# Attention contexts normalized between two 32x32 block turns on VectorE instead of between TensorE turns

## The reference

```python
def _mha(q, k, v, wq, wk, wv, wo):
    B, S, d = q.shape
    dh = d // H
    qh = (q @ wq).reshape(B, S, H, dh)
    kh = (k @ wk).reshape(B, S, H, dh)
    vh = (v @ wv).reshape(B, S, H, dh)
    scores = jnp.einsum('bqhd,bkhd->bhqk', qh, kh) / jnp.sqrt(jnp.asarray(dh, q.dtype))
    attn = jax.nn.softmax(scores, axis=-1)
    ctx = jnp.einsum('bhqk,bkhd->bqhd', attn, vh).reshape(B, S, d)
    return ctx @ wo
...
for c in range(NUM_NOD):
    ...
    o = _mha(q, k, v, Wq[c], Wk[c], Wv[c], Wo[c])
    nodes[c] = act_w[c] * o + q
...
return _layernorm(out, ln_g, ln_b)
```

## Time and profile before

| | us |
|---|---|
| runs | 2162.97, 2163.7, 2166.92; median 2163.7 |
| the profiled execution, first to last instruction | 2167.6 |
| TensorE busy, matmuls | 2020.1 (93%), 14620 instructions |
| VectorE busy | 1686.2 (78%), 2918 instructions |
| ScalarE busy | 1374.7 (63%), 2687 instructions |
| GpSimd busy | 1112.7 (51%), 1509 instructions |

### The profile page before, as it was taken

How to read it: one execution, slowest core, us unless ns; L and a number is a source line. 1 busy time by engine, 2 the same in 40 slices (tenths; PEclk the granted TensorE clock), 3 DMA queues, 4 the chain that set the end, 5 groups by cost and what they waited for, 6 DMA issues and landing times. The chain is left out here.

```text
span 2167.6 us, 40610 instructions
## 1 busy us (share of the span) xinstructions
PE 2020.1 (93%) x14620; PEld 1506.8 (70%) x14620; DVE 1686.2 (78%) x2918; ACT 1374.7 (63%) x2687; POOL 1112.7 (51%) x1509
## 2 busy tenths in 40 slices
PE   6999999986999995999999988699999999999878
PEld 4677777754887773677777755577877877877745
DVE  5777777765888875777777765499999999999974
ACT  1677777763777773677777653467586685685633
POOL 3555555623767764555555512345736647556423
PEclk8899999997999997999999997899999999999989
DMA  4655566530000003555555515000000000000000
GB/s 133 148 149 147 146 148 149 145 106 1 2 2 2 2 2 78 151 149 146 149 145 150 150 31 200 1 1 1 1 1 1 1 1 0 1 0 1 1 15 20
DMA packets 147750, 144.94 MB, mean 67 GB/s; under 512 B 14048, under 2 KB 106976, under 8 KB 146912
## 3 DMA queue, kind: packets, MB, share of 16 engines
q1 hardware_dynamic: 127968, 132.91, 22.4%
q10 hardware_dynamic: 19584, 9.44, 2.4%
HBM read 94.07 MB, written 38.80 MB: 61 GB/s over the span
## 5 line engine op out<-in xcount | busy, mean ns | idle before, releaser
L606 DVE TENSOR_REDUCE sb_f_mx<-ps_f_s 128x2 f32<-128x512 f32 x768 | 506.4, 686 | 216.5 <-PE ps_f_s L354 215.6
L530 ACT ACTIVATE sb_f_pt<-ps_f_t 128x1024 f32<-128x1024 f32 x384 | 382.1, 1023 | 114.9 <-issue 56.2
L1954 POOL TENSOR_TENSOR sb_mb_h<-sb_mb_h 128x512 f32<-128x512 f32 x128 | 165.0, 1310 | 303.4 <-DVE sb_mb_h L1837 302.3
L354 PE MATMUL ps_f_s<-sb_f_stack 96*128 96x256 bf16 x1536 | 286.5, 279 | 22.1 <-DMA sb_f_stack<-f_scr 14.1
L1832 DVE TENSOR_TENSOR_SCAN sb_mb_h<-sb_mb_da,sb_mb_h 128x1024 f32<-128x1024 f32 x128 | 304.4, 2418 | 2.7 <-ACT sb_mb_da L1692 2.7
L1503 PE MATMUL ps_mb_f<-sb_mb_fc,sb_mb_cw 128*128 128x256 f32 x1280 | 286.8, 381 | 6.7 <-ACT sb_mb_fc L1705 6.6
L1503 PEld LDWEIGHTS ps_mb_f<-sb_mb_fc,sb_mb_cw 128*128 128x128 f32 x1280 | 239.7, 190 | 41.4 <-ACT sb_mb_fc L1705 8.9
L371 PE MATMUL ps_f_t<-sb_f_stack 128*128 128x256 bf16 x1536 | 232.9, 274 | 6.3 <-ACT sb_f_pt L530 3.3
L1692 ACT ACTIVATE sb_mb_da<-sb_mb_dl,sb_mb_an 128x255 f32<-128x255 f32 x512 | 211.0, 496 | 31.3 <-DVE sb_mb_h L1832 30.7
L354 PEld LDWEIGHTS ps_f_s<-sb_f_stack 96*128 96x128 bf16 x1536 | 140.7, 99 | 109.7 <-issue 41.3
L427 PE MATMUL ps_f_a<-sb_f_pt,sb_f_v 128*32 128x256 f32 x3072 | 188.8, 387 | 1.6 <-ACT sb_f_v L579 1.6
(11 more groups left out here) (252 smaller groups left out, 4132.7 us busy)
## 6 DMA issues: line engine op xcount, KB each, us to landing
f_scr<-sb_f_parts SPq DMA_DIRECT2D x96, 384.0 KB, 2.7
sb_f_stack<-f_scr SPq DMA_DIRECT2D x192, 192.0 KB, 3.0
sb_f_stack<-f_scr SPq DMA_DIRECT2D x192, 128.0 KB, 3.1
sb_f_stack<-f_scr SPq DMA_DIRECT2D x192, 64.0 KB, 3.3
sb_f_stack<-sb_f_mrow ACTq DMA_DIRECT2D x96, 96.0 KB
sb_mb_cw<-in_cw SPq DMA_DIRECT2D x1, 5120.0 KB, 19.4
sb_prep_wn<-in_wn SPq DMA_DIRECT2D x6, 512.0 KB, 7.7
sb_m_w<-in_w SPq DMA_DIRECT2D x6, 256.0 KB, 3.1
```

Source lines behind the costliest of these rows:

```text
L354: last = nc.tensor.matmul(s_bank[j % 2][:, h, :], stack[0:ROWS, a.n % STACKS, 0, g * GROUP + pair * 2 + h, half * P:(half + 1) * P], stack ...
L530: nc.scalar.activation(pt[:, e.two, g, half, :, :], t_bank[i % 2][:, :, :], ACT.Exp).then_inc(s["pt_sb"], 1)
L606: nc.vector.tensor_reduce(mx[:, a.two, half, head:head + 2], s_bank[j % 2][:, :, :], AX.X, ALU.max)\
L1954: nc.gpsimd.tensor_tensor(hb[:, c, 0:2, :], hb[:, c, 0:2, :], hb[:, c, 2:4, :], ALU.add).then_inc(s["half_sb"], 1)
```

## The change

The contexts are not turned on TensorE any more. `by_token(u)` on VectorE reads the context bank with one block turn (each 32x32 block by itself) into `ct`, so that the partitions are 32 tokens of each of four heads, and takes the reciprocal of the 16 sums per partition. GpSimd multiplies (`normalize(u)`) into `cn`, and `by_dim(o)` on VectorE turns the blocks back into `cf`. ScalarE's copies `cs` and `cf` and TensorE's `context_tok` and `context_back` are gone. Heads are dealt to slots in another order, so the columns of Wv and the rows of Wo are permuted on the host. The turn of the maxima becomes a plain product with the identity into an fp32 bank. Waits follow the new buffers. A step's item u, not item o of the next step, is now read from the bank.

```diff
-        cs = k.sb(f"{tag}_cs", [P, NG, N], ctx)
-        rsum = k.sb(f"{tag}_rsum", [P, NG, 2, GROUP], ctx)
-        cn = k.sb(f"{tag}_cn", [P, 2, NG, GROUP, DH], ctx)
+        ct = k.sb(f"{tag}_ct", [P, NG, N // SLOT, SLOT], ctx)
+        rsum = k.sb(f"{tag}_rsum", [P, NG, N // SLOT], ctx)
+        cn = k.sb(f"{tag}_cn", [P, N // SLOT, NG, DH], ctx)
...
-        mrow_ps = act_bank[0:MAXROWS, N:N + N // 2].bitcast(BF16)
+        mrow_ps = act_bank[0:MAXROWS, N:2 * N]
...
-                if f.n > OUT_LAG - 1:
-                    pe.wait_ge(s["cn_sb"], f.n - OUT_LAG + 1)
+                if f.n > OUT_LAG:
+                    pe.wait_ge(s["node_sb"], f.n - OUT_LAG)
...
             def values(m, e, o):
 
                 if o:
-                    pe.wait_ge(s["cf_sb"], o.n + 1)
+                    pe.wait_ge(s["ct_sb"], o.n + 1)
                 elif e:
                     pe.wait_ge(s["v_sb"], e.n)
                     if m:
@@ -400,8 +400,9 @@
                 if m:
                     pe.wait_ge(s["mp_sb"], m.n + 1)
                     for half in range(2):
-                        last = nc.tensor.transpose(mrow_ps[:, half * P:(half + 1) * P],
-                                                   mp[:, half, :, :].rearrange("p t h -> p (t h)"), w.identb[:, :])
+                        last = nc.tensor.matmul(mrow_ps[:, half * P:(half + 1) * P],
+                                                mp[:, half, :, :].rearrange("p t h -> p (t h)"), w.identb[:, :],
+                                                start=True, stop=True)
...
-                    pe.wait_ge(s["cf_sb"], u.n)
+                    pe.wait_ge(s["ct_sb"], u.n)
...
-                                                    v[:, u.two, half, g * GROUP + h, :],
+                                                    v[:, u.two, half, h * NG + g, :],
...
-            def context_tok(o):
-
-                pe.wait_ge(s["cs_sb"], o.n + 1)
-                if o.n:
-                    pe.wait_ge(s["node_sb"], o.n)
-                else:
-                    pe.wait_ge(s["qf_sb"], OUT_LAG)
-                for g in range(NG):
-                    for half in range(2):
-                        last = nc.tensor.transpose(mix_bank[:, (2 * g + half) * P:(2 * g + half + 1) * P],
-                                                   cs[:, g, half * P:(half + 1) * P], k.ident[:, :])
-                last.then_inc(s["ct_ps"], 1)
-
-            def context_back(o):
-
-                pe.wait_ge(s["cn_sb"], o.n + 1)
-                for half in range(2):
-                    last = nc.tensor.transpose(act_bank[:, half * P:(half + 1) * P],
-                                               cn[:, half, :, :, :].rearrange("p g h e -> p (g h e)"), k.ident[:, :])
-                last.then_inc(s["cb_ps"], 1)
...
                 if u:
                     scores_t(u, 3)
-                if o:
-                    context_tok(o)
                 if a:
                     scores(a, 0)
...
                     scores_t(e, 1)
-                if o:
-                    context_back(o)
                 if f and step >= EXP_LAG:
                     queries(f)
...
-                if o:
-                    act.wait_ge(s["ctx_ps"], o.n + 1)
-                    if o.n:
-                        act.wait_ge(s["ct_ps"], o.n)
-                    nc.scalar.activation(cs[:, :, :].rearrange("p g n -> p (g n)"), act_bank[:, :], ACT.Copy)\
-                        .then_inc(s["cs_sb"], 1)
+                u = ffn_item(step, SUM_LAG)
                 if u:
                     exponent(u, 3)
...
-                if o:
-                    act.wait_ge(s["cb_ps"], o.n + 1)
-                    if o.n:
-                        act.wait_ge(s["out_ps"], o.n)
-                    nc.scalar.activation(cf[:, :], act_bank[:, 0:N], ACT.Copy).then_inc(s["cf_sb"], 1)
...
-            def normalize(o):
-
-                dve.wait_ge(s["ct_ps"], o.n + 1)
-                ct = mix_bank[:, :].rearrange("p (g a h e) -> p g a h e", g=NG, a=2, h=GROUP)
-                nc.vector.reciprocal(rsum[:, :, :, :], ct[:, :, :, :, SUMROW]).then_inc(s["rsum_sb"], 1)
-                dve.wait_ge(s["rsum_sb"], o.n + 1)
+            def by_token(u):
+
+                dve.wait_ge(s["ctx_ps"], u.n + 1)
+                if u.n:
+                    dve.wait_ge(s["cn_sb"], u.n)
+                nc.vector.transpose(ct[:, :, :, :].rearrange("p g j e -> p (g j e)"), act_bank[:, :]).then_inc(s["ct_sb"], 1)
+                dve.wait_ge(s["ct_sb"], u.n + 1)
+                nc.vector.reciprocal(rsum[:, :, :], ct[:, :, :, SUMROW]).then_inc(s["rsum_sb"], 1)
+
+            def by_dim(o):
+
+                dve.wait_ge(s["cn_sb"], o.n + 1)
                 if o.n:
-                    dve.wait_ge(s["cb_ps"], o.n)
-                for half in range(2):
-                    last = nc.vector.tensor_tensor(
-                        cn[:, half, :, :, :], ct[:, :, half, :, 0:DH],
-                        rsum[:, :, half, :].rearrange("p g (h o) -> p g h o", o=1).broadcast_to([P, NG, GROUP, DH]),
-                        ALU.mult)
-                last.then_inc(s["cn_sb"], 1)
+                    dve.wait_ge(s["out_ps"], o.n)
+                nc.vector.transpose(cf[:, :], cn[:, :, :, :].rearrange("p j g e -> p (j g e)")).then_inc(s["cf_sb"], 1)
...
-                if o:
-                    normalize(o)
                 for j in range(8):
                     if a:
                         row_max(a, j)
+                    if o and j == 0:
+                        by_dim(o)
+                    if u and j == 5:
+                        by_token(u)
...
+            def normalize(u):
+
+                pool.wait_ge(s["rsum_sb"], u.n + 1)
+                if u.n:
+                    pool.wait_ge(s["cf_sb"], u.n)
+                nc.gpsimd.tensor_tensor(cn[:, :, :, :].rearrange("p j g e -> p g j e"), ct[:, :, :, 0:DH],
+                                        rsum[:, :, :].rearrange("p g (j o) -> p g j o", o=1).broadcast_to([P, NG, N // SLOT, DH]),
+                                        ALU.mult).then_inc(s["cn_sb"], 1)
...
                 if f:
                     split(f)
+                if u:
+                    normalize(u)
...
+    heads = np.arange(D).reshape(NG, GROUP, DH).transpose(1, 0, 2).reshape(-1)
...
-                              np.stack([by_dim(a["L0_ffn_Wq"]), by_dim(a["L0_ffn_Wk"]), a["L0_ffn_Wv"].transpose(1, 0, 2),
-                                        a["L0_ffn_Wo"].transpose(1, 0, 2), we[:, 0].transpose(1, 0, 2)], 2)], 2),
+                              np.stack([by_dim(a["L0_ffn_Wq"]), by_dim(a["L0_ffn_Wk"]),
+                                        a["L0_ffn_Wv"].transpose(1, 0, 2)[:, :, heads],
+                                        a["L0_ffn_Wo"].transpose(1, 0, 2)[heads], we[:, 0].transpose(1, 0, 2)], 2)], 2),
```

7 lines of the change are left out of this document (3 added, 4 removed).

## The result

| | us |
|---|---|
| before, run beside it | 2163.34 median (2162.56 to 2166.92, 4 runs) |
| changed kernel | 2204.76 median (2199.29 to 2207.09, 4 runs) |
| ratio | 1.0181, 95% interval 1.0169 to 1.0194 |
| the profiled execution of the changed kernel | 2199.29, span 2197.2 |

The change makes the kernel 1.8% slower, 41 us by the medians. The forecast was 2187 us, in a range of 2168 to 2210: the sign and the mechanism held, the size was too small by 18 us. The 2175 to 2200 us that the forecast's own terms spanned do not hold 2204.76. It lies in the part up to 2210 that was added for a held-up product on GpSimd, which did not happen in the plain steps, so the range held partly by luck. Two further sets of runs of the same kernel gave 1.0181 (1.0164 to 1.0198) and 1.0169 (1.0155 to 1.0183), 39.6 and 36.4 us.

A forecast was written before the change was run, and what follows sets the result against it. TensorE, working without a gap, was taken as the bound. Plain steps' 8.6 us plus 0.4 and 3 made 12 us a phase, 24 in both, less 1, added to 2163.7: 2187 us, range 2168 to 2210.

The forecast's parts named there:

- a held-up product on GpSimd: Rival: GpSimd's context product takes 2.41 us and delays the turn of the maxima by 0.2 us; 2203 us, 5%.
- TensorE was the bound, and 0.65 us comes off it: TensorE fills the 8.72 us feed-forward step; dropping context turns (0.44 us) and turns back (0.21 us) saves 0.65 us.
- the 8.07 of the prediction: Feed-forward step in us if removing TensorE's turns were the only effect, down from 8.72 us.
- C+0.88: C is the start of scores 6; TensorE was to wait for scores 0 from 0.88 us after it.
- Nothing for the maxima's products: On TensorE, the two products turning the maxima keep their size as plain products: no time gained or lost.
- VectorE's chain in front of scores 0: Block turn, reciprocal and row maximum of scores 6 delay scores 0 from C+1.32 to C+1.74; step 0.21 us longer.
- The steps' 17.2 us: Forecast cost of the plain steps in both phases: 41 a phase, each 0.21 us longer.
- 1 us less for early steps: Early steps that now wait for a DMA would find it landed: 1 us off the total.
- GpSimd's product and the second block turn hidden: Product of 0.73 us and turn of about 0.4 us cost nothing while TensorE's wait before scores 0 covers them.
- The three steps with scores and the final turn, 0.4 us together: Per phase, the three steps having both scores and the final turn were to cost some 0.4 us together.
- a falling clock: Rival: TensorE's clock falls because of the new idle time, up to 8 us more a step; 2227 us, 2%.
- The end of a phase, 3 us within 1 to 5: In steps without scores, layer-norm additions stand behind the first block turn and delay the output: 3 us a phase.

The follow-up runs named there:

- experiment 9: Changed kernel with block turn and reciprocal behind row maximum 7, later GpSimd product, queries before scores 0, keys behind scores_t 1, layer-norm additions first at phase ends: 2118.02 us.
- experiments 6: Changed kernel with the products of queries and keys moved in front of scores 0 on TensorE: 2160.84 us, ratio to before 0.9979.
- experiment 5: Kernel before the change with only the maxima's rows turned by plain products with the identity into fp32 PSUM: 2164.27 us, ratio 0.9994.
- experiment 7: Changed kernel with the layer norm's additions in front of the contexts' block turn in steps without scores: 2185.24 us, ratio to before 1.0089.
- experiment 2: Changed kernel with only the reciprocal moved, behind row maximum 7 instead of in front of row maximum 6: 2182.96 us, ratio to before 1.0080.

## Why the prediction was nearly right, step by step

- **TensorE was the bound, and 0.65 us comes off it.** Held: in experiment 9 the step is 8.24 us, which is the 8.07 of the prediction and the 0.16 us that scores 2 still waits. TensorE is ready for scores 0 at C+0.88, as predicted: in experiments 6 and 9 the queries' products start at C+0.89. The idle time of 0.78 us counts only from C+1.05, where the record of scores_t 3 ends. Counted by starts, the changed kernel loses 0.95 us in front of scores 0, and 8.07 + 0.95 is its step of 9.01 us to within 0.01.
- **Nothing for the maxima's products**: held (experiment 5).
- **VectorE's chain in front of scores 0**: the mechanism held, C+1.83 instead of C+1.74. The turn started at C+0.14, the reciprocal at C+0.89 instead of C+0.84, row maximum 6 at C+1.06 instead of C+1.00, and scores 0 0.77 us behind its start instead of 0.74. The largest term is the turn with its hand-over, 0.75 instead of 0.71 us. The row that I took for its length, the row maximum of the same size, was 5% under the turn's 0.717 us (0.68). The steps' 17.2 us became 21.5: **this term was too small by 4 us**. The sum's 1 us less for early steps was about right: the stretch up to the first context is 0.6 us shorter, and the steps of before that took longer than their neighbours are mostly gone.
- **GpSimd's product and the second block turn hidden**: held, 0.62 instead of 0.73 us; the second turn 0.43 us. No wait stands at the turn of the maxima in the changed kernel's plain steps. The rival of a held-up product was wrong for it. It looked only at the row maxima beside the product, though, and not at the additions at a phase's end, which read two buffers in SBUF: there VectorE's addition took longer and not the product (experiment 7). And the cover is thin: 0.26 us later it was gone in six steps of a phase (experiment 2).
- **The three steps with scores and the final turn, 0.4 us together**: too small. In the first profile they are 2.1 and 2.0 us longer. TensorE's wait there grew from 1.26 to 1.81 us and the clock fell behind it. The prediction dismissed a falling clock because the one stretch of the earlier trace rows that idled had kept 1.00. That was right for the plain steps, where 0.78 us of idle time in 9.01 left it at 1.00 in every profile, and wrong for these. The price I had given it, up to 8 us a step, was far too high: one fall costs about 1.4 us (12.34 against 10.89).
- **The end of a phase, 3 us within 1 to 5**: the place was right, the additions behind the block turn. The steps without scores grew by 2.8 us in the first phase and 1.9 in the second, and what lies behind the phases by another 2.3 and 2.9 us on the mean of the profiles. So the ends of a phase make about 5 instead of 3 us, at the edge of the range given. The 3.89 us taken for the additions and the centring became 4.27 (496.87 to 501.14), since one of them now runs beside GpSimd's product.
- **The sum**: 23 us forecast, 35 by the means of the profiles, 36 to 41 by the medians. Roughly 4 us of the gap are the plain steps, 3 the steps with scores and the final turn, 4 the ends. The few us between 35 and 41 are executions with more or fewer falls of the clock; that this is all of it was not shown.

## What to carry to other kernels

When work is moved off the bounding engine, look at who waits for the engine that receives it, and at what stands behind it there: what counts is the distance from the last thing it waits for to the first thing the bounding engine waits for, set against the time at which that engine would ask for it. A moved instruction of 0.25 us can cost 0.26 us a step while an engine stands idle a quarter of the time. The same instructions placed behind that handoff made a loss of 1.8% into a gain of 0.4%, and 2.2% with TensorE's order fitted to it. To size such a chain take distances between starts, and a longer one for an instruction that reads what the last one wrote. In the ramp of a pipeline, compare with what the ends would be without the new wait, not with what they were.
